# A graph network on one core: the node stage of the convolution taken into the loop over edges

## The reference

```python
h = silu(edge_scalars @ fc_w1 / sqrt(8)) * SILU_NORM
w_a, w_b, w_c, w_d = split(h @ fc_w2 / 8)
xg0, xg1 = y0[edge_src], y1[edge_src]
mids = concat([w_a * xg0 * ea0, w_b * (xg1 . ea1) / sqrt(3),
               (w_c * xg0)[:, :, None] * ea1[:, None, :], (w_d * ea0)[:, :, None] * xg1])
agg = segment_sum(mids, edge_dst) / sqrt(20)               # 640 sums per node
out = c_s * self_connection(x) + c_x * lin2(agg)           # the node stage begins here
x1 = layernorm(x + out)
xp = x1 @ lin_w                                            # and what the attention reads:
a_i, a_j = xp . att_i, xp . att_j                          # the node stage ends here
out = elu(layernorm(attention(xp, a_i, a_j, src, dst)) * ln_w + ln_b) + x1
result = layernorm(x1 + out)
```

## Time and profile before

| | us |
|---|---|
| median of three runs | 4669.1 |
| the profiled execution, its own time | 4664.99 |
| its span, first to last instruction | 4663.6 |
| PE busy | 4158.5 (89%) |
| DVE busy | 3623.9 (78%) |
| POOL busy | 3212.8 (69%) |
| ACT busy | 1445.1 (31%) |
| loop over edges | some 95 to 2204 |
| node stage | 2204 to 2513.5 |

### The profile page before, as it was taken

How to read it: one execution, slowest core, us unless ns; L and a number is a source line. 1 busy time by engine, 2 the same in 40 slices (tenths; PEclk the granted TensorE clock), 3 DMA queues, 4 the chain that set the end, 5 groups by cost and what they waited for, 6 DMA issues and landing times. The chain is left out here.

```text
span 4663.6 us, 115274 instructions
## 1 busy us (share of the span) xinstructions
PE 4158.5 (89%) x33992; PEld 2693.8 (58%) x33992; DVE 3623.9 (78%) x10643; ACT 1445.1 (31%) x3213; POOL 3212.8 (69%) x3384
## 2 busy tenths in 40 slices
PE   6988888888888888887997899999988999899997
PEld 5444444444444444443996666777666776666675
DVE  3777777777777777775775888888888888888887
ACT  4111111111111111111553344444444444444444
POOL 3777777777777777775003777777777777777774
PEclk8999999999999999999997888788888788888888
DMA  7444444444444444445774444444444444444443
GB/s 267 133 131 132 131 132 131 132 131 131 131 132 132 131 132 131 132 131 138 281 297 166 122 124 125 123 123 125 122 124 124 124 124 122 125 123 123 125 122 88
DMA packets 375419, 649.80 MB, mean 139 GB/s; under 512 B 130024, under 2 KB 249914, under 8 KB 373548
## 3 DMA queue, kind: packets, MB, share of 16 engines
q0 software_dynamic: 161120, 444.76, 34.6%
q1 hardware_dynamic: 214220, 204.13, 13.5%
HBM read 546.90 MB, written 101.68 MB: 139 GB/s over the span
## 5 line engine op out<-in xcount | busy, mean ns | idle before, releaser
L1995 POOL DMA_INDIRECT ord_xg<-xpa_rows,ord_meta x1666 | 1596.5, 958 | 510.9 <-issue 472.9
L869 POOL DMA_INDIRECT sub_xg<-y_rows,sub_meta x1668 | 1595.3, 956 | 510.5 <-issue 462.8
L2063 PE MATMUL ord_a<-ord_xg,ord_sel 128*128 128x264 f32 x3332 | 1144.5, 478 | 115.4 <-DVE ord_xg L2426 115.2
L919 PE MATMUL sub_a<-sub_mids,sub_sel 128*32 128x128 f32 (+1 forms) x13344 | 998.5, 305 | 228.8 <-DVE sub_mids L1081 221.2
L2063 PEld LDWEIGHTS ord_a<-ord_xg,ord_sel 128*128 128x128 f32 x3332 | 723.0, 238 | 254.3 <-DVE ord_xg L2426 122.9
L1081 DVE TENSOR_TENSOR sub_mids<-sub_w,sub_xg 128x384 f32<-128x384 f32 x1668 | 844.2, 548 | 0.0
L919 PEld LDWEIGHTS sub_a<-sub_mids,sub_sel 128*32 128x32 f32 x13344 | 438.1, 109 | 692.3 <-DVE sub_mids L1081 586.3
L1076 DVE TENSOR_TENSOR sub_mids<-sub_w,sub_xg 128x256 f32<-128x256 f32 x834 | 354.3, 425 | 522.0 <-DMA sub_xg<-y_rows,sub_meta 373.3
L989 ACT ACTIVATE sub_agg_s<-sub_a 128x256 f32<-128x256 f32 x556 | 213.9, 385 | 1618.6 <-PE sub_a L936 1543.3
L899 PE MATMUL sub_w<-sub_fc,sub_ht 64*128 64x256 f32 x3336 | 586.7, 429 | 0.0
L2426 DVE TENSOR_TENSOR ord_xg<-ord_xg,ord_prob 128x1024 f32<-128x1024 f32 x476 | 510.3, 1072 | 0.0
(11 more groups left out here) (183 smaller groups left out, 4153.4 us busy)
## 6 DMA issues: line engine op xcount, KB each, us to landing
sub_sum_rows<-sub_agg_s SPq DMA_DIRECT2D x556, 64.0 KB
mid_rows<-sub_sum_rows SPq DMA_DIRECT2D x14, 2240.0 KB, 8.7
sub_xg<-y_rows,sub_meta POOLq DMA_INDIRECT x1668
ord_xg<-xpa_rows,ord_meta POOLq DMA_INDIRECT x1666
ord_x_rows<-x_rows SPq DMA_DIRECT2D x119, 128.0 KB, 2.2
out_dram<-ord_res SPq DMA_DIRECT2D x119, 128.0 KB
xpa_rows<-mid_proj SPq DMA_DIRECT2D x14, 924.0 KB, 5.3
lin_xt<-in_x_t_dram SPq DMA_DIRECT2D x14, 896.0 KB, 9.9
```

Source lines behind the costliest of these rows:

```text
L869: nc.gpsimd.indirect_dma_start(xg[:, b, k], None, y, bass.IndirectOffsetOnAxis(ids[:, b, 0, k:k + 1], 0))\
L919: mm = nc.tensor.matmul(a[ROWS * m:ROWS * (m + 1), 0:w].rearrange("p (q f) -> p q f", f=MUL), sel[:, b, k, m], of, start=(j == 0), stop=False,
L1995: nc.gpsimd.indirect_dma_start(xg[:, b, k], None, xpa, bass.IndirectOffsetOnAxis(ids[:, b, k:k + 1], 0))\
L2063: mm = nc.tensor.matmul(psum_a[b % 2][:, 0:WIDE], sel[:, b, k], xg[:, b, k], start=(k == 0), stop=(k == TILES - 1 and not has(i, b, -1)), ...
```

## The change

The stage `end_convolution` is no longer called on this path. Its work is done inside `convolve_in_order`, in pairs of node tiles (256 nodes) instead of batches of seven. There are 49 pairs. Pair i-1 is worked on in turn i, for i from 1 to 45, in PSUM bank h, which it shares with the hidden layer; the remaining four follow behind the loop in the banks that are free there. Two turns are peeled in place of one.

- SyncE: `load_x` (x_t and x of the pair) before the stores of the third group, then at the end of the turn `load_sums`, which waits for all stores of the earlier turns, and `store_pair` of the pair before (x1, xpa, att).
- PE: `hidden` moves behind `weigh` of pairs 0 and 1; `turn_sums` in group 0 (pairs 4 and 5), `add_self` in group 1 (pair 2), `turn_normed` and `project` in group 2 (pairs 2, 3, 4).
- DVE: both folds after the fifth pair of group 0, `add_x` and `moments` after the last two pairs of group 1, `normalise` after the second pair of group 2.
- ACT: the copies and the square root between `copy_out`s.
- Before the loop one more array is loaded (`pair_factor`), and a condition `late` joins those under which this path is taken: the nodes of pair i-1 must lie below the first destination of turn i.

The products of a pair and their number are those of two tiles of the old stage. The diff, cut to its core:

```diff
+TURN_SUBS = SUB_TURN * GROUP_SUBS
+SUB_TURNS = math.ceil(SUB_GROUPS / SUB_TURN)
+NODE_PAIR = 2 * P
+NODE_PAIRS = NODES_PAD // NODE_PAIR
+LOOP_PAIRS = SUB_TURNS - 2
+TAIL_PAIRS = NODE_PAIRS - LOOP_PAIRS
...
-def in_subs(eng, body, peeled=1):
+def in_subs(eng, body, peeled=2):
...
+        def with_pair(i):
+            return type(i) is not int or 0 < i <= LOOP_PAIRS
+        tail = [(LOOP_PAIRS + e, (e + 1) % TAIL_PAIRS, LOOP_PAIRS + 1 if e == TAIL_PAIRS - 1 else 1, (e + 1) % 2,
+                 e // 2 + 1 + (LOOP_PAIRS if e % 2 else 0)) for e in range(TAIL_PAIRS)]
...
+                def load_x(n, buf, past):
+                    if past is not None:
+                        wait_alone(sp, z_done, past)
+                        wait_alone(sp, pre_done, past)
+                    sp.dma_start(node_xt[:, buf].rearrange("p c j n -> p c (j n)"),
+                                 pair_xt_dram[:, :, bass.ds(n * NODE_PAIR, NODE_PAIR)]).then_inc(x_in[buf], 16)
+                    sp.dma_start(node_x[:, buf].rearrange("p j f -> p (j f)"), pair_rows(io["x"], n))\
+                        .then_inc(x_in[buf], 16)
+                def load_sums(n, buf, subs, past):
+                    if past is not None:
+                        wait_alone(sp, turned, 2 * past)
+                    wait_alone(sp, stored, stored_subs(subs))
+                    sp.dma_start(node_rows[:, buf].rearrange("p j q f -> p (j q f)"), pair_rows(sums, n))\
+                        .then_inc(sums_in[buf], 16)
+                def store_pair(n, buf):
+                    wait_alone(sp, out_done, n + 1)
+                    sp.dma_start(pair_rows(x1, n), out[:, buf].rearrange("p j f -> p (j f)")).then_inc(x1_out[buf], 16)
+                    wait_alone(sp, p_copied, 2 * n + 2)
+                    sp.dma_start(pair_rows(xpa, n), proj[:, buf].rearrange("p j f -> p (j f)"))\
+                        .then_inc(proj_out[buf], 16)
+                    sp.dma_start(pair_rows(att, n), proj_a[:, buf].rearrange("p j f -> p (j f)"))\
+                        .then_inc(proj_out[buf], 16)
...
+                        if b == SUB_TURN - 1 and with_pair(i):
+                            load_x(i - 1, 0, None if is_pair(i, 1) else i - 1)
+                        if b == 0 and is_pair(i, SUB_TURNS - 1):
+                            for n, buf, times, _, _ in tail:
+                                load_x(n, buf, LOOP_PAIRS if times > 1 else None)
                         if has(i, b, -SUB_TURN):
                             store(g - SUB_TURN, b)
-                    if type(i) is int and i > 0:
+                    if with_pair(i):
+                        load_sums(i - 1, 0, TURN_SUBS * i, None if is_pair(i, 1) else i - 1)
+                        if not is_pair(i, 1):
+                            store_pair(i - 2, 0)
+                    if is_pair(i, SUB_TURNS - 1):
+                        for n, buf, _, _, _ in tail[0:-1]:
+                            load_sums(n, buf, TURN_SUBS * i, None)
+                        store_pair(LOOP_PAIRS - 1, 0)
                         for g in range(SUB_TURN * i, SUB_GROUPS):
                             store(g, g % SUB_TURN)
-                        sp.wait_ge(stored, stored_subs(SUBS))
+                        load_sums(tail[-1][0], tail[-1][1], SUBS, LOOP_PAIRS)
+                        for n, _, _, buf, _ in tail:
+                            store_pair(n, buf)
...
+                def turn_sums(n, j, buf, bank):        # PE: waits folded, four transposes
+                def add_self(n, buf, times, bank):     # PE: waits turned_copied and x_in, 2 x 6 products
+                def turn_normed(n, buf, bank):         # PE: waits out_done, four transposes
+                def project(n, j, bank):               # PE: waits t_copied, two products of 272 columns
+                def bank_of_hidden(i, b, u, g):
+                    if (b, u) == (0, 4):
+                        pe.wait_ge(silu_done, 2 * g + 4)
+                        turn_sums(i - 1, 0, 0, psum_h)
+                    if (b, u) == (0, 5):
+                        pe.wait_ge(turned_copied, 2 * i - 1)
+                        turn_sums(i - 1, 1, 0, psum_h)
+                    if (b, u) == (1, 2):
+                        pe.wait_ge(silu_done, 2 * g + 4)
+                        add_self(i - 1, 0, i, psum_h)
+                    if (b, u) == (2, 2):
+                        pe.wait_ge(silu_done, 2 * g + 4)
+                        turn_normed(i - 1, 0, psum_h)
+                    if (b, u) == (2, 3):
+                        project(i - 1, 0, psum_h)
+                    if (b, u) == (2, 4):
+                        pe.wait_ge(p_copied, 2 * i - 1)
+                        project(i - 1, 1, psum_h)
+                def free_hidden(i, b):
+                    if b == 0 and with_pair(i) and not is_pair(i, 1):
+                        pe.wait_ge(p_copied, 2 * i - 2)
+                    if b == 1 and with_pair(i):
+                        pe.wait_ge(turned_copied, 2 * i)
+                    if b == 2 and with_pair(i):
+                        pe.wait_ge(pre_done, i)
...
-                            if u in (1, 3) and more:
-                                hidden(g + 1, after, after_i, u // 2, False)
...
+                            if u < 2 and more:
+                                if u == 0:
+                                    free_hidden(i, b)
+                                hidden(g + 1, after, after_i, u, False)
+                            if with_pair(i):
+                                bank_of_hidden(i, b, u, g)
...
+                def with_products(i, b, u):
+                    if (b, u) == (0, 4):
+                        fold(i - 1, 0, 0, i, is_pair(i, 1))
+                        fold(i - 1, 1, 0, i, is_pair(i, 1))
+                    if (b, u) == (1, 4):
+                        add_x(i - 1, 0, i, psum_h, is_pair(i, 1))
+                    if (b, u) == (1, 5):
+                        moments(i - 1)
+                    if (b, u) == (2, 1):
+                        normalise(i - 1, 0, None if is_pair(i, 1) else i - 1, is_pair(i, 1))
...
-                convolve_in_order(nc, io, c, y, sub_sums, kept)
-                end_convolution(nc, io, c, sub_sums, x1, xpa, att, 5, kept)
+                convolve_in_order(nc, io, c, y, sub_sums, x1, xpa, att, kept)
```

More of the change, by code:

```diff
@@ L725, in convolve_edges, with convolve_in_order @@
             rounds(nc, c, one_round)
-def in_subs(eng, body, peeled=1):
+def in_subs(eng, body, peeled=2):
     in_turns(eng, SUB_GROUPS, SUB_TURN, body, peeled)
-def convolve_in_order(nc, io, c, y, sums, kept):
+def convolve_in_order(nc, io, c, y, sums, x1, xpa, att, kept):
     PAIRS = SUB_TILES // 2
@@ L994, in turn @@
                         silu(0, 0, 1, True)
+                    first = is_pair(i, 1)
+                    past = None if first else i - 1
                     for b in range(SUB_TURN):
@@ L1086, in products, with fold @@
                     a.then_inc(mids_done, 2)
+                def fold(n, j, buf, times, first):
+                    dve.wait_ge(sums_in[buf], 16 * times)
+                    if not first:
+                        dve.wait_ge(turned, 2 * n + j - 1)
+                    f, rows = fold_rows[:, j], node_rows[:, buf, j]
+                    nc.vector.tensor_reduce(f[:, 0:MUL], rows[:, 1:4, 0:MUL].rearrange("p q f -> p f q"), AX, ALU.add)
+                    nc.vector.tensor_copy(f[:, MUL:].rearrange("p (q f) -> p q f", f=MUL), rows[:, 1:4, MUL:])\
+                        .then_inc(folded, 1)
@@ new lines, in add_x @@
+                def add_x(n, buf, times, bank, first):
+                    if not first:
+                        dve.wait_ge(out_done, n)
+                    dve.wait_ge(z_done, n + 1)
+                    dve.wait_ge(x_in[buf], 32 * times)
+                    for j in range(2):
+                        z, x, o = bank[:, j * FEAT:(j + 1) * FEAT], node_x[:, buf, j], pre[:, j]
+                        a = c["pair_factor"][:, bass.ds(2 * n + j, 1)]
+                        nc.vector.scalar_tensor_tensor(out=o[:, 0:MUL], in0=z[:, 0:MUL], scalar=a, in1=x[:, 0:MUL],
+                                                       op0=ALU.mult, op1=ALU.add)
+                        last = nc.vector.scalar_tensor_tensor(
+                            out=o[:, MUL:].rearrange("p (u c) -> p c u", c=3),
+                            in0=z[:, MUL:].rearrange("p (c u) -> p c u", c=3), scalar=a,
+                            in1=x[:, MUL:].rearrange("p (u c) -> p c u", c=3), op0=ALU.mult, op1=ALU.add)
+                    last.then_inc(pre_done, 1)
@@ L1108, in turn @@
                                     select(g + 1, after, k)
+                            if with_pair(i):
+                                with_products(i, b, u)
                 in_subs(dve, turn)
+                for e in range(TAIL_PAIRS):
+                    n, buf, times, out_buf, stores = tail[e]
+                    if e == 0:
```

(8 more changed lines are left out.)

196 lines of the change are left out of this document (181 added, 15 removed).

## The result

The changed kernel takes 4835.1 us, the median of four runs (4832.4 to 4839.1), beside 4668.6 (4667.4 to 4671.5) for the kernel before: a ratio of 1.0356, 95% interval 1.0338 to 1.0374. It is slower, and above the predicted range.

A forecast was written before the change was run, and what follows sets the result against it. SyncE's in-order queue was taken to bind the changed loop at 51.4 us a turn. Loop +267 and tail -257 gave +10 on the profiled 4665.0; with 4.1 for the median, 4679 us, range 4611 to 4779.

The forecast's parts named there:

- The loop is bound by POOL's gathers, and SyncE is nearly as full.: Loop before the change: 36 gathers fill the 45.40 us turn; SyncE's own work takes 43.83.
- SyncE's own work, 43.83 + 6.7 = 50.5.: SyncE's queue in the loop: six DMAs, their waits and an exposed landing add 6.7 us, making 50.5 a turn.
- Traffic, +0.9.: Loop stores on SyncE: the pair's 1.73 MB adds 0.9 us a turn, within bounds of -0.7 and +2.
- the first rival: SyncE's store chain gets quicker as gathers thin out: a turn of 50.0 us, 4611 in all; chance 0.15.
- The tail, 112 us, -257.: From SyncE's last turn to the attention's first load: 112 us in place of 369, a gain of 257.
- So SyncE doesn't wait for them, and the queue stays the bound.: Loop: the third group's copies are ready 37 us after the sums land, SyncE asks 43 after, so it never waits.
- "1 us" of slack: Loop, inside the cooled-PE rival: PE's slack towards SyncE where it waits for the gathers of a turn's third group.
- That cushion is used once: POOL in the loop may run 8 tiles ahead; its gathers' sums are ready some 5 us early, a margin used once.
- One pause a turn of 5 to 6 us in the gathers.: Sign of being right: POOL's loop gathers stay 1.26 us apart, with a single pause of 5 to 6 us each turn.
- Wrong: ... SyncE's waits on `copied` or on gathers of several us (then PE or DVE is): Sign of being wrong: SyncE in the loop waits several us for copies or gathers, making PE or DVE the bound.
- DVE's lumps, 48 to 49 us for PE and DVE.: Loop: DVE's four lumps before products hold up PE, 48 to 49 us a turn; as rival 4526, chance 0.03.
- The fold's pause cools PE: 53.4 a turn, 4779.: Rival: PE's clock falls at each fold, about 2 us a turn come through, 53.4 a turn, 4779; chance 0.22.

The follow-up runs named there:

- e4: Kernel before, with only the six DMAs of a pair and their waits added to SyncE's queue; 4876.1 us, ratio 1.0421.
- e1: Changed kernel with each group's four stores issued ahead of the load of the group three later, turns 1 to 45; 4610.2 us, ratio 0.9859.
- e7: Changed kernel with twelve unused products on PE ahead of a pair's first transposes, in the wait for the fold; 4786.3 us, ratio 1.0232.
- e10: Changed kernel with stores ahead of loads, sums loaded one group earlier, x loads and result stores issued by ACT; 4529.3 us, ratio 0.9703.
- e6: Changed kernel with a pair's sums loaded one group of stores earlier, behind the x loads, from turn 8 on; 4644.2 us, ratio 0.9947.
- three cuts at three places: Changed kernel, separately: stores ahead of loads (ratio 0.9859), gathers 14 tiles ahead in place of 8 (0.9876), sums loaded one group earlier (0.9947).
- the control: Kernel before with stores ahead of loads in the loop; 4667.6 us, ratio 0.9998.
- e8: Changed kernel with stores ahead of loads, and x loads and the three result stores issued by ACT; 4585.2 us, ratio 0.9826.

## Why the prediction was wrong, point by point

- *The loop is bound by POOL's gathers, and SyncE is nearly as full.* Right, and so was the consequence that the queue can't take six more DMAs for nothing: e4 shows it alone.
- *SyncE's own work, 43.83 + 6.7 = 50.5.* Measured 49.7 (e4) and 49.4 (after, less its wait for gathers). Right but for 0.8 us, and 0.7 of that is one misread row: the att store of the earlier trace rows holds seven tiles (56 KB) and is issued in 1.05 us, the pair's holds two (16 KB) and is issued in 0.35.
- *Traffic, +0.9.* Wrong: the sum without it is already above what was measured, and the waits for landings are 640.3/347 = 1.85 us where they were 1.89. The bound at -0.7 was the nearer. With e4's chain the forecast would have been 45 x 4.3 - 3 - 257 = -66, near the first rival, and e1 comes close to that world: -1.41%, some 66 us below its own before. That the two agree to the microsecond is luck, since e1 also has the waits for copies.
- *The tail, 112 us, -257.* Measured 120.5, -248.5. The fourth x load, forecast at +18.5, goes out at 2580.90, +22.2. The three sums loads, due behind the last landing at +62, go out at 2627.57, +68.9, so the twelve stores are late by some 3 us more, and the four pairs by the rest. The attention's own +6.4 was put at nothing.
- *"So SyncE doesn't wait for them, and the queue stays the bound."* This is the step that failed. It was made for the copies, and there it held (5.3 us in all). For the gathers before the third group the text had only "1 us" of slack, inside a rival and without a working: a chain of 50.4 beside a queue of 51.4. With the queue at its real 49.7 that chain would already have bound. And it was too short, because of *"That cushion is used once"*: behind its restart POOL was taken to run at 1.26 a gather. Its 16 gathers take 21.91 us at full clock in place of 18.9 (e7), and 23.20 behind a cold PE; the restart comes 4.31 us after the fold at full clock and 5.17 cold, where 4.7 was forecast. The chain is 52.2 us at full clock and 54.6 as it ran. 50.4 + 0.5 + 4.3 would give 55.2, so the 50.4 itself was some 0.6 too long.
- *One pause a turn of 5 to 6 us in the gathers.* Four instead, 4.01 + 1.83 + 0.69 + 2.67 = 9.2 us. *DVE waits 3 to 5 us at the fold.* 175.6/35 = 5.0. *"Wrong: ... SyncE's waits on `copied` or on gathers of several us (then PE or DVE is)"*: the wait on gathers came, 5.2 us a turn, but it is no sign that PE or DVE is the bound by itself; it is one link of a chain that runs through all of them.
- *DVE's lumps, 48 to 49 us for PE and DVE.* With everything else out of the way (e10) 47.4. Good, and not the bound.
- *The fold's pause cools PE: 53.4 a turn, 4779.* The right place, the right engine, the right wait on SyncE, and nearly the right price: 2 us a turn, where e7 shows 2.4. It was put on top of the queue's 51.4, where the chain at full clock is 52.2. So it fell 1.2 us a turn short, 45 x 1.2 = 54 of the 56 us between 4779 and 4835. Without any cooling the kernel would take about 4835 - 45 x 2.4 = 4727 (an estimate from e7's turns at 1.00), still slower than before. The tail is 8.5 us longer than forecast, where this rival had 10; how much of it is the clock was not measured.

That the order on SyncE closes the chain is shown, by three cuts at three places and by the control. The cuts also warm PE, to 0.98 or 0.99, so by themselves they don't tell the chain from the clock; e7 does, with 53.3 us a turn at 0.98, where e6 has 50.0 at the same clock, and with 52.2 in its turns at 1.00 against 49.4 in those of e1. That the wait of 2.67 us at full clock is due to the pair's own products on PE is read from the timeline; no run moves them to another place.

## What to carry to other kernels

When prefetch loads and result stores share one in-order queue, and a new step reads those results back inside the loop, draw the closed chain through the queue (gathers, load, stores, read-back, fold, products, gathers) and sum it as a chain of its own; a slack of 1 us found by walking a schedule with constant rates is no slack. Give the price of a cold PE to whichever chain is the longest, and not to the one that was taken to bind. Then try the cheap cuts first: moving one load behind the stores was worth some 230 us, and nothing in the kernel where that chain doesn't exist. Opening one more chain may gain little while another stands beside it: on top of e1, ACT's queue gave 0.3% and the earlier read-back cost 0.5%, both together gave 1.6%.

## What of the hardware was not expected

- Behind a wait of 4 to 5 us, once in 54.6, PE is granted 1.2 GHz for some 7 us (8.7 us at 0.61 are 6.8 at 0.5 and the rest at 1), though it is busy for 39.7 of the 40.3 us that follow. With waits of up to 1.1 us the turn of the kernel before has 1.00. With some 2.9 us of extra products in the wait (e7) the clock is 1.00 in 11 turns of 27, and lower in the others of the same program.
- A sub's store (two DMAs, 64 and 16 KB) directly behind the 640 KB load of sums is waited for as long as 5.7 us (e6, with 512 KB of x before it) and 6.1 (e8, where x is loaded from ACT's queue). Directly behind the 512 KB of x alone it is 3.0 at most (after).
- The att store is issued in 0.35 us in the loop (16 KB) and in 1.05 in the old node stage (56 KB).
